# Four heads' negated row maxima turned as twelve shared rows, a second home for the context, a new table of tasks and written-out passes in a fused decoder layer

## The reference, cut to what matters

```python
Q = proj(query, wq_w, wq_b); K = proj(key, wk_w, wk_b); V = proj(value, wv_w, wv_b)
#   query = x, key = value = ctx_1024, 16 heads of 16 columns
scores = jnp.einsum('bhqd,bhkd->bhqk', Q, K) * scale
scores = jnp.where(causal, scores, -jnp.inf)
attn = jax.nn.softmax(scores, axis=-1)
out = jnp.einsum('bhqk,bhkd->bhqd', attn, V)
x = _layernorm(x + (out @ wo_w.T + wo_b), axis=-1)
```

## Time and profile before

| | |
|---|---|
| median of three runs | 717.75 us |
| profiled execution | 715.91 us, its span 713.8 us |
| PE busy | 595.8 us (83%) |
| DVE, ACT, POOL busy | 361.1, 276.8, 193.0 us |
| recurrence and MLP | 0 to about 198 us |
| attention, four passes | about 198 to 457 us |
| last norm, logits, top-k | 457 to 518 us |
| experts, final norm | 518 to 713.8 us |

### The profile page before, as it was taken

One profiled execution on the slowest core, in us unless ns is written; L12 is line 12 of the kernel. 1 busy time (PEld: TensorE's weight loads), 2 busy tenths in 40 slices (PEclk: granted clock), 3 DMA queues, 4 the chain that ended last, 5 costly groups with the idle time before them and its releaser, 6 DMA issues.

```text
span 713.8 us, 11692 instructions
## 1 busy us (share of the span) xinstructions
PE 595.8 (83%) x3966; PEld 346.4 (49%) x3966; DVE 361.1 (51%) x791; ACT 276.8 (39%) x456; POOL 193.0 (27%) x251
## 2 busy tenths in 40 slices
PE   3799999999979888999999988720099999999945
PEld 2557667574845445565555554310045545545522
DVE  4673534143166765675687565159623334334435
ACT  3142241404127655667666566110033333333203
POOL 2251403131121131122123223010134444443224
PEclk9899999999969999999999999865589999999976
DMA  7794000010522322152233461048069999998755
GB/s 238 253 377 154 2 0 0 0 60 1 169 77 79 133 87 91 63 187 78 75 105 132 148 191 74 0 170 371 7 212 382 396 398 394 404 397 289 185 165 217
DMA packets 41159, 120.69 MB, mean 169 GB/s; under 512 B 3697, under 2 KB 25889, under 8 KB 38049
## 3 DMA queue, kind: packets, MB, share of 16 engines
q1 hardware_dynamic: 35536, 113.17, 43.1%
q0 software_dynamic: 4608, 6.29, 4.3%
q10 hardware_dynamic: 976, 0.73, 0.4%
HBM read 96.07 MB, written 22.02 MB: 165 GB/s over the span
## 4 chain that ended last, share of the span: by engine, by line
PE 70%; DVE 13%; issue 5%; ACT 5%; DMA 5%; POOL 1%; SPq 0%; ACTq 0%; DVEq 0%; POOLq 0%
PE PS L1824 12%; PE PS L1534 7%; PE PS L1543 6%; PE PS L1687 5%; PE PS L1618 4%; PE PS L1700 4%; PE PS L1856 4%; PE PS L1659 4%; PE PS L1837 3%; DVE Mx L1022 3%; PE PS L1505 2%; PE PS L1610 2%; PE PS L1522 2%; PE PS L1850 2%; PE PS L1655 2%
## 5 line engine op out<-in xcount | busy, mean ns | idle before, releaser
L1022 DVE TENSOR_REDUCE Mx<-PS 128x1 f32<-128x384 f32 (+3 forms) x176 | 102.9, 635 | 53.0 <-PE PS L1659 52.6
L1371 ACT ACTIVATE arena<-PS 128x512 f32<-128x512 f32 (+1 forms) x176 | 90.7, 560 | 46.5 <-PE PS L1687 45.0
L742 POOL TENSOR_SCALAR_AFFINE_SELECT arena<-arena 128x512 f32<-128x512 f32 x64 | 40.8, 637 | 178.9 <-ACT arena L1371 178.9
L1687 PE MATMUL PS<-arena 99*128 99x512 bf16 (+3 forms) x256 | 62.9, 308 | 11.6 <-ACT arena L1371 9.5
L1659 PE MATMUL PS<-arena 96*128 96x128 bf16 (+3 forms) x256 | 63.5, 307 | 0.0
L1534 PE MATMUL PS<-arena 128*128 128x512 f32 x128 | 56.1, 593 | 3.2 <-ACT arena L1286 1.6
L1543 PE MATMUL PS<-arena 128*128 128x256 f32 x256 | 55.9, 379 | 0.0
L1443 ACT ACTIVATE X<-X 128x512 f32<-128x512 f32 x48 | 29.4, 630 | 62.0 <-DVE X L1192 62.0
L1543 PEld LDWEIGHTS PS<-arena 128*128 128x128 f32 x256 | 48.6, 190 | 6.6
L1185 DVE COPY X<-PS 128x512 f32<-128x512 f32 x24 | 16.6, 692 | 68.9 <-PE PS L1824 68.9
L1700 PE MATMUL PS<-arena 128*32 128x128 f32 (+3 forms) x512 | 48.5, 449 | 1.1 <-POOL arena L742 1.0
(11 more groups left out here) (205 smaller groups left out, 1013.4 us busy)
## 6 DMA issues: line engine op xcount, KB each, us to landing
ring_a<-experts SPq DMA_DIRECT2D x12, 2048.0 KB, 15.8
arena<-experts SPq DMA_DIRECT2D x12, 2048.0 KB, 17.6
ring_a<-experts SPq DMA_DIRECT2D x12, 512.0 KB, 12.2
sums<-zrow SPq DMA_DIRECT2D x3, 2048.0 KB, 20.4
arena<-pieces SPq DMA_DIRECT2D x32, 192.0 KB
arena<-experts SPq DMA_DIRECT2D x12, 512.0 KB, 14.3
arena<-pieces SPq DMA_DIRECT2D x32, 128.0 KB
pieces<-arena SPq DMA_DIRECT2D x4, 768.0 KB, 3.7
```

What stands on the lines that cost most here:

```text
L742: pool.affine_select(out=pb[j % 2][:, :, 0:P], in_=pb[j % 2][:, :, 0:P], compare_op=ALU.is_ge, fill=0.0, base=0, pattern=[[0, GH], [1, P]] ...
L1022: dve.tensor_reduce(Mx[:, g % 2, i, heads[0]:heads[-1] + 1], bank(score_banks[(g * NSH + u) % 3])[:, 0:len(heads) * w] .rearrange("p (h n) ...
L1371: act.activation(pb[j % 2][:, heads[0]:heads[-1] + 1, 0:w], bank(exp_banks[(g * NSH + n) % 2])[:, 0:len(heads) * w] .rearrange("p (h n) -> ...
L1687: mm = pe.matmul(bank(exp_banks[(g * NSH + n) % 2])[:, a * w:(a + 1) * w], KTs[0:SX, g * GH + h, j * P:(j + 1) * P], QTs[0:SX, g * GH + h, ...
```

## The change

Six edits, all in the attention:

- **Twelve shared rows.** PE turns the 12 pieces (4 heads x 3) of a tile at once, 4 transposes for a group instead of 16, into one spare bank. ACT copies the same 12 rows to all four heads of `QTs`, in two instructions as before. So `KTs` can't hold ones: for head h it holds 1 in the three rows of head h and 0 in the other nine. A table `own` (12 rows by 4 heads, from a DVE reduction of the identity) is made for that, and POOL copies it with four tensor copies in place of four memsets. The contraction of `shifted` has 108 rows instead of 99.
- **Two homes for the context.** `cTs[b % 2]`, with a semaphore each; a pass's context is loaded one pass earlier.
- **Table of tasks.** Nearly all tasks change places; `value` 1 is made in the pass before, and for pass 0 ahead of the attention.
- **CUTS** of slot 2: the last score bank moves behind the values of slot 1.
- **Passes written out**: no loops, so passes 1 and 2 have constants where registers were computed.
- The wait for both spare banks ahead of the loop is gone.

```diff
-SX = SK + NPC
+SX = SK + GH * NPC
-CUTS = [(3, 3), (4, 4), (3, 4), (0, 0)]
+CUTS = [(3, 3), (4, 4), (3, 3), (0, 0)]
@@ TASKS
-    (0, 0): ([("value", 1, 0)], [], [], []),
-    (0, 1): ([("query_in", 0, 1)], [], [], [("query_in", 1, 1)]),
-    (0, 2): ([], [], [("heads", 1, -1)], [("query", 0, 1), ("query", 1, 1)]),
-    (1, 0): ([], [], [], [("split_q", 0, 1)]),
-    (1, 1): ([("key", 0, 1)], [], [("key", 1, 1)], []),
-    (1, 2): ([("split_k", 0, 1), ("output", 0, -1)], [], [], []),
-    (1, 3): ([("output", 1, -1)], [], [("stats", 0, -1)], []),
-    (2, 1): ([("norm", 0, -1)], [("value", 0, 1)], [], []),
-    (2, 2): ([], [("turn", 0, -1)], [("turn", 1, -1)], []),
-    (3, 0): ([("heads", 0, 0), ("bias", 0, 0)], [], [], []),
-    (3, 2): ([], [], [("logits", 0, -1)], []),
+    (0, 0): ([("query_in", 0, 1), ("query_in", 1, 1)], [], [], []),
+    (0, 2): ([], [("bias", 0, 0)], [], []),
+    (0, 3): ([], [("query", 0, 1)], [("query", 1, 1)], [("heads", 1, -1)]),
+    (1, 0): ([("key", 0, 1)], [], [], []),
+    (1, 1): ([("output", 0, -1)], [("split_q", 0, 1)], [("key", 1, 1)], []),
+    (1, 3): ([], [], [("output", 1, -1), ("split_k", 0, 1)], [("stats", 0, -1)]),
+    (2, 0): ([("value", 0, 1)], [], [], []),
+    (2, 1): ([], [("norm", 0, -1)], [], [("heads", 0, 0)]),
+    (2, 3): ([], [("turn", 0, -1), ("turn", 1, -1)], [], []),
+    (3, 0): ([("logits", 0, -1)], [], [], []),
+    (3, 3): ([("value", 1, 1)], [], [], []),
@@ SP
-                sp.wait_ge(vpr.s, vpr.before(b, 2))
-                sp.dma_start(cT, ctx_v[b]).then_inc(c_in.s, 16)
+                if b >= 2:
+                    sp.wait_ge(vpr.s, vpr.now(b - 2, 2))
+                sp.dma_start(cTs[b % 2], ctx_v[b]).then_inc(c_in[b % 2].s, 16)
...
             for b in range(B - 1):
-                context_in(b + 1)
                 split_out(b + 1)
                 if b + 2 < B:
                     tokens_in(b + 2)
+                    context_in(b + 2)
                 for g in (0, 1):
                     group_in(b + 1, g)
@@ POOL, DVE
-                pool.memset(KTs[SK:SX, GH * g:GH * g + GH, :], 1.0).then_inc(ones, 1)
+                pool.tensor_copy(KTs[SK:SX, GH * g:GH * g + GH, :],
+                                 own[SK:SX, :].unsqueeze(2).to_broadcast([SX - SK, GH, T]))\
+                    .then_inc(ones, 1)
+            dve.tensor_reduce(own[SK:SX, :], ident[SK:SX, SK:SX]
+                              .rearrange("p (h c) -> p h c", h=GH), AX.X, ALU.add)\
+                .then_inc(owns, 1)
@@ ACT minus_max
+                act.wait_ge(ntp.s, ntp.now(b, g + 1))
                 for m in range(2):
-                    act.wait_ge(ntp.s, ntp.now(b, 2 * g + m + 1))
                     act.activation(QTs[SK:SX, GH * g + 2 * m:GH * g + 2 * m + 2, :],
-                                   spare(m).bitcast(BF16)[SK:SX, :]
-                                   .rearrange("p (h n) -> p h n", h=2), ACT.Copy)\
+                                   wide(spare(0).bitcast(BF16)[SK:SX, 0:T], 2), ACT.Copy)\
@@ PE minus_max
-                for m in range(2):
-                    o = take(m, nte, nte.now(b, 2 * g + m + 1)).bitcast(BF16)
-                    for h in range(2):
-                        for i in range(TT):
-                            mm = pe.transpose(o[SK:SX, (TT * h + i) * P:(TT * h + i + 1) * P],
-                                              nst[:, g % 2, i, 2 * m + h, :], identb[:])
-                    mm.then_inc(ntp.s, 1)
+                o = take(0, nte, nte.now(b, 2 * g + 2)).bitcast(BF16)
+                for i in range(TT):
+                    mm = pe.transpose(o[SK:SX, i * P:(i + 1) * P],
+                                      nst[:, g % 2, i].rearrange("p h c -> p (h c)"), identb[:])
+                mm.then_inc(ntp.s, 1)
@@ POOL, DVE, ACT, PE
-            with pe.Fori(1, B - 1) as b:
+            for b in range(1, B - 1):
                 slots(b, pe_slot)
```

More of the change, by code:

```diff
@@ L176, in build @@
         nst = sb("nst", [P, 2, TT, GH, NPC], BF16)
+        own = sb("own", [P, GH])
         zrow = sb("zrow", [P, D])
@@ L226, in build @@
         prepared = used[0]
-        cT = carve(KT * T).rearrange("p (k n) -> p k n", k=KT)
         kp = carve(NPC * KT * T // 2).bitcast(BF16).rearrange("p (c k n) -> p c k n", c=NPC, k=KT)
         kr = carve(KT * T).rearrange("p (k n) -> p k n", k=KT)
+        cTs = [carve(KT * T).rearrange("p (k n) -> p k n", k=KT) for _ in range(2)]
         over = ring_a[:, 0, :]
@@ L339, in build @@
         rs3 = signal("rs3", 2)
-        c_in = signal("c_in", 1, 16)
+        c_in = [signal(f"c_in{n}", 1, 16) for n in range(2)]
         xs_in = signal("xs_in", 1, 16)
@@ L355, in build @@
         ones = sem("ones")
+        owns = sem("owns")
         vpr = signal("vpr", 2)
@@ L360, in build @@
         mneg = signal("mneg", NG * 4)
-        ntp = signal("ntp", NG * 2)
+        ntp = signal("ntp", NG)
         nte = signal("nte", NG * 2)
@@ L507, in _ @@
                 sp.dma_start(sums_all[a], wide(zrow[:], B * TT)).then_inc(zsum, 16)
-            sp.sem_inc(c_in.s, 16)
+            for g in c_in:
+                sp.sem_inc(g.s, 16)
             sp.sem_inc(xs_in.s, 16)
@@ L565, in _ @@
             context_in(0)
+            context_in(1)
             split_out(0, query_first=False)
@@ L717, in _ @@
             pool.wait_ge(vset, 2)
+            pool.wait_ge(owns, 1)
             pool.wait_ge(m1.s, m1.now(B - 1, MT))
@@ L752, in _ @@
             slots(0, pool_slot, first=True)
-            with pool.Fori(1, B - 1) as b:
+            for b in range(1, B - 1):
                 slots(b, pool_slot)
@@ L1030, in negate @@
                 dve.wait_ge(mxs.s, mxs.now(b, NSH * (g + 1)))
-                dve.wait_ge(ntp.s, ntp.now(b, 2 * (g - 1)) if g >= 2
-                            else ntp.before(b, 2 * (NG + g - 1)))
+                dve.wait_ge(ntp.s, ntp.now(b, g - 1) if g >= 2 else ntp.before(b, NG + g - 1))
                 dve.tensor_scalar(d[:, :, :, 0], m, -1.0, None, ALU.mult).then_inc(mneg.s, 1)
@@ L1110, in _ @@
             slots(0, dve_slot, first=True)
-            with dve.Fori(1, B - 1) as b:
+            for b in range(1, B - 1):
                 slots(b, dve_slot)
@@ L1416, in _ @@
             slots(0, act_slot, first=True)
-            with act.Fori(1, B - 1) as b:
+            for b in range(1, B - 1):
                 slots(b, act_slot)
@@ L1621, in pe_key @@
             def pe_key(b, m):
-                pe.wait_ge(c_in.s, c_in.now(b, 1))
-                pe_features(take(m, ksd, ksd.now(b, m + 1)), wkv_s[:, :, m * P:(m + 1) * P], cT)\
+                pe.wait_ge(c_in[b % 2].s, c_in[b % 2].now(b // 2, 1))
+                pe_features(take(m, ksd, ksd.now(b, m + 1)), wkv_s[:, :, m * P:(m + 1) * P], cTs[b % 2])\
                     .then_inc(kpr.s, 1)
@@ L1786, in _ @@
             slots(0, pe_slot, first=True)
-            for k in range(2):
-                pe.wait_ge(*read_by[k])
-            with pe.Fori(1, B - 1) as b:
-                read_by.update({m: (nte.s, nte.now(b, m + 1)) for m in range(2)})
+            for b in range(1, B - 1):
                 slots(b, pe_slot)
-            read_by.update({m: (nte.s, nte.now(B - 1, m + 1)) for m in range(2)})
             slots(B - 1, pe_slot, last=True)
```

2 lines of the change are left out of this document (1 added, 1 removed).

## The result

The changed kernel takes 721.74 us (median of 8 runs, 718.27 to 723.45) against 716.92 us for the kernel before on the same chip (8 runs, 712.33 to 720.21). The ratio is 1.0069, 95% interval 1.0039 to 1.0099: slower by 0.4% to 1.0%. The forecast was 715.8 us, 2 us faster. The measured 721.7 lies in its range, but the direction was wrong.

What follows compares the result with a forecast made beforehand. The prediction took the middle passes to be bound by a PE stream with few holes. It summed -19.5 us of savings, +12 for late key pieces and +5.5 for the clock to -2, so 715.8 us, range 704 to 725.

Steps and rivals of the forecast that it cites:

- +17.5: Passes 0 to 2: +12 us for PE's waits for late key pieces, +5.5 for the clock falling behind them.
- the sum of -19.5: Whole attention without the key pieces: opening 0, pass 0 -5.5, passes 1 and 2 -4.5 each, pass 3 -5 us.
- 3.7 becomes 0.3: Middle passes: moved tasks and the single spare bank cut PE's waits from 3.7 to 0.3 us, 3.4 saved.
- the 1.9 us taken off in pass 3: Pass 3, group 3: waits for POOL (1.0) and DVE (0.9) go because `bias` and `heads` 0 have left.
- opening: Ahead of pass 0: `value` 1 comes in, `query_in` takes its old place; net 0 us, bounds -1 and +2.
- Transposes: Group boundaries: 12 fewer save 0.67 us of PE, but ACT's copy limits three to 0.2; 1.3 us per middle pass.
- The reads: Ends of passes 0 to 2: key pieces land late, PE stands about 4 us each, +12 us in all.
- the 0.8 for the context: SP's queue: the context's load issued ahead of group 0's reads adds 0.8 us to PE's wait, bounds 0 and 3.
- A chain of fixed latencies: From `split_k` to group 0's landing: 16.7 us that faster passes and free DMA bandwidth don't shorten.
- The clock: Behind the three waits for pieces: PE's clock falls to 1.2 GHz, costing 5.5 us, bounds 0 and 12.
- the key pieces decide the pass: Rival (20%), PE's wait for group 0 in slot (3, 0): 6 us waits, dearer clock falls, 725 us.
- The rival at 6%: Rival (6%), whole change: the twelve-row copy is slower, or tasks only move waits and holes stay; 717.8 us.

Runs made afterwards that it cites:

- e5: The changed kernel with twelve reads of 16 rows per group in place of six of 48, 32 and 16: 707.92 us, ratio 0.988 to the kernel before.
- e11: e5 with `value` 1 made in slot (0, 0) of its own pass again: 714.51 us, ratio 0.996 to the kernel before.
- e10: e5 with the old CUTS of slot 2, the last score ahead of slot 1's values: 704.32 us, ratio 0.984 to the kernel before.
- e12: e5 with `bias` back in slot (3, 0): 711.49 us, ratio 0.989 to the kernel before.
- e1: The changed kernel with `split_k` back in slot (1, 2): 710.05 us, ratio 0.991 to the kernel before.
- e2: The kernel before with `split_k` moved behind the second `output` in slot (1, 3): 728.46 us, ratio 1.018.
- e6: The changed kernel with the context's load behind the reads of groups 0 and 1: 720.69 us, ratio 1.006 to the kernel before.
- e4: The changed kernel with the old TASKS and CUTS; twelve rows, two homes and written-out passes stay: 715.09 us, ratio 0.997 to the kernel before.
- e3: The kernel before with its passes written out and the wait ahead of the loop gone: 715.57 us, ratio 1.001.
- e9: The kernel before with only the reads changed to twelve DMAs of 16 rows per group: 714.99 us, ratio 0.9975.

## Why the prediction was wrong, by its own steps

The clean split is e5 against the changed kernel: the same program but for the reads. Both were timed against the kernel before, so the ratios can be subtracted: 1.0069 - 0.9875 = 1.9%, 13.9 us, is what the late pieces cost with their clock (the profiled spans say 716.5 - 701.9 = 14.6, of which 13.8 lie in passes 0 to 2). What remains, 0.9875 - 1 = -1.25% or -9 us (95% interval -0.65% to -1.85%, some -5 to -13; spans: -11.9), is the change without them. The forecast had +17.5 and -19.5.

**The step that failed is the sum of -19.5, and in it above all "3.7 becomes 0.3" and the 1.9 us taken off in pass 3.** By terms, from the spans of before and e5:

| term | forecast | measured |
|---|---|---|
| opening | 0 | -0.5; the move of `value` 1 itself +1.7 (e11), the MLP's last part began 1.9 us sooner in that execution |
| pass 0 | -5.5 | -3.3 |
| passes 1, 2 | -4.5 each | -3.2, -2.9 |
| pass 3 and what follows | -5 | -2.0 |

- *Transposes.* PE's work fell by 2.67 us a pass, 4 x 0.67 as worked out. And ACT's copy did take the place of 4 x 0.67 - 1.3 = 1.4 us of it: three waits of 0.46 for L1369. This step was right.
- *The copy of twelve rows.* L1369 takes 1008 ns a piece, L1358 took 1010. Right.
- *Waits.* Those for the exponentials went, as did that for L986. But I priced the fillers at the places where they came to and not where they left. `bias`, `norm`, `turn` and `output` were all put closer to DVE's and ACT's own deadlines; what is left in a middle pass beside L1369 is 0.9 for `nst` in slot (2, 3), 0.4 + 0.2 for L998, a spare bank's last reader, and 0.2 + 0.2: some 1.9 us in place of 0.5. That closes the sum: -1.3 for the boundaries and -1.8 for the waits give -3.1, measured -3.2 and -2.9. Of these waits only the 0.9 was traced to its cause: e10 takes it away by the old CUTS, and the pass stays as long. That `norm`, `turn` and `output` make the others is read from the table, and no run moved them. The middle pass is bound by more than the one wait that a view names.
- *Pass 0.* Two waits for `nst` of 2.28 and 1.10 us became 1.80 each, and not 1.2; 0.7 of each is the new CUTS, which the forecast gave no price (e10).
- *Pass 3.* I took off 1.9 us for waits of POOL and DVE and kept 2.1 of ACT's exponentials. Measured, both of the former stayed nearly whole, and 3.0 of ACT's; the wait for DVE's L1062 (before, L1051) belongs to the last turn of results at the pass's end, which no task's move could reach (waits from 396 to 460):

```profile
PE PS L1679 <- DVE nst L1051: 3.9, 2, 3.0
PE PS L1695 <- ACT arena L1381: 3.0, 6, 1.1
PE PS L1708 <- POOL arena L751: 0.9, 2, 0.7
PE PS L1607 <- DVE Y L1062: 0.9, 1, 0.9
```

- *Pass 3, the turning in slot (0, 3).* The wait for `nst` became 2.96 us, where the kernel before has

```profile
409.19 0.89 PE L1671 MATMUL PS<-identb,nst 128*3 128x128 bf16 x13 [0.66 <-DVE nst L1040]
```

  Of the 2.96, 1.15 go when `bias` moves back (e12). The remaining 1.81 are as long as the other waits for `nst` with no task ahead of the turning (1.80 in pass 0 and in e11); `heads`, which stood ahead of this turning, now stands behind it. That this is the cause was not tried.
- *The reads.* Forecast: `split_k` ends 4.7 us later and PE is due 1.0 sooner, so 13.5 us lie between them; the pieces land 17.5 us behind `split_k` (16.7, and 0.8 for the context's load); PE stands some 4 us, three times. Measured in pass 2: 1.8 later and 2.9 sooner within the pass, 14.5 us between them, the pieces 17.5 us behind `split_k`, and waits of 2.3, 3.4 and 3.1 us in the three passes, 8.8 in sum for 12. The mechanism and the place were right (e1, e2); the 0.8 for the context was not (e6). "A chain of fixed latencies" was wrong: where PE waited for it (after, e1, e2, e4, e6) it took 17.2 to 19.7 us, and DMAs of 16 rows take 5.5 us out of it (e5). That the share of 0.19 in the earlier trace rows is three engines was read there. The Trainium skill ("DMA: Bandwidth & Descriptors", section "Why a DMA increments its semaphore by 16 and not by 1") has a DMA run on the largest number of engines, up to 16, that divides the outermost dimension of both sides. The trace agrees: reads split into 16 rows land in 2.3 us, at a share of up to 0.49. I drew from it only that these reads could not go faster, not that others could.
- *The clock.* Forecast 5.5 us. At the three waits there were 6.8, 3.4 and 3.4 us at half clock. Against e5 the three passes are 3.8, 5.1 and 4.9 us longer, 13.8 in sum, so what comes on top of the 8.8 us of waits is some 5: right.
- *Written-out passes.* Worth nothing, as forecast (e3, 0.999 to 1.004).

Of the rivals, "the key pieces decide the pass" gave 725 and asked for waits of 6 us, which never came; the time went its way because the gain was half of what I took, not because the price was higher. The rival at 6% says that "tasks only move waits about", which is what took half of the gain; it stood there at its full strength (717.8 us), and no part of it in the forecast. That the measured time lies inside the stated range says nothing for the sum. What would have told me: in the kernel before, PE's listed waits of 3.7 us were all of its idle time (3.8), and of a table that moves sixteen tasks to another slot I had followed PE's queue and not DVE's and POOL's.

**Left open.** While PE stands for the pieces, the DMA engines are not idle: their share is 0.77 and 0.63, SP having issued the writes of `x_rows` and `sums` right behind the reads (383.83). Whether these delay the last read was not tried. Nor is it known why some executions have falls of the clock in passes 0 and 3 and others do not; runs of one kernel spread by about 1%, the slower ones mostly with a lower mean clock. Where the 0.25% of e9 comes from is open too. The opening is one candidate: e2 and e3, whose opening is that of the kernel before, stood 2.8 us for the pieces ahead of pass 0, and e4 3.97, where e9 stood 1.70; no run tried it.
